# Experts: table rows made four tiles at a time, gate steps moved between the first shared units, first weight matrix split early in a job

## What is computed

```python
logits = relu(xf @ Wr1 + br1) @ Wr2 + br2
gates = softmax(logits)
tg, ti = top_k(gates, 2)
tg = softmax(tg / 2)
out = silu(xf @ Ws1 + bs1) @ Ws2 + bs2          # shared expert
for e in range(8):
    h = silu(xf @ We1[e] + be1[e]) @ We2[e] + be2[e]
    out = out + sum(tg * (ti == e)) [:, None] * h
```

## Time and profile before

| | us |
|---|---|
| median of 3 timed runs | 3277.19 (3273.32 to 3281.86) |
| profiled execution, whole | 3266.33 |
| its span (first to last instruction) | 3264.6 |
| PE busy | 2611.5 (80%) |
| DVE busy | 2268.8 (69%) |
| ACT busy | 1770.8 (54%) |
| POOL busy | 1493.4 (46%) |

### The profile page before, as it was taken

How to read it: one execution, slowest core, us unless ns; L and a number is a source line. 1 busy time by engine, 2 the same in 40 slices (tenths; PEclk the granted TensorE clock), 3 DMA queues, 4 the chain that set the end, 5 groups by cost and what they waited for, 6 DMA issues and landing times. The chain is left out here.

```text
span 3264.6 us, 38830 instructions
## 1 busy us (share of the span) xinstructions
PE 2611.5 (80%) x11128; PEld 1659.1 (51%) x11128; DVE 2268.8 (69%) x4031; ACT 1770.8 (54%) x3051; POOL 1493.4 (46%) x1600
## 2 busy tenths in 40 slices
PE   6788129989989989877788069958988888886999
PEld 5666014334334334226666057745655555553787
DVE  5477247999999999986477244557777778773443
ACT  2477036655655656523477045525777766764554
POOL 3765546887887888864764700021121112110000
PEclk7999659999999999996899579978999999997999
DMA  2045112222222222211145110000000000001000
GB/s 83 14 130 125 52 56 61 70 71 70 72 69 71 72 69 71 73 57 51 27 138 111 52 39 1 0 11 1 1 1 1 2 2 1 1 1 36 7 7 13
DMA packets 99367, 146.02 MB, mean 45 GB/s; under 512 B 12892, under 2 KB 50524, under 8 KB 98980
## 3 DMA queue, kind: packets, MB, share of 16 engines
q1 hardware_dynamic: 82052, 98.41, 9.9%
q0 software_dynamic: 16608, 44.78, 5.8%
q10 hardware_dynamic: 512, 0.53, 0.1%
HBM read 124.78 MB, written 18.87 MB: 44 GB/s over the span
## 5 line engine op out<-in xcount | busy, mean ns | idle before, releaser
L1548 POOL TENSOR_TENSOR a_hc<-a_H,a_cb 128x512 f32<-128x512 f32 x512 | 623.2, 1225 | 191.8 <-DVE a_H L1464 157.0
L1281 PE MATMUL a_Y<-a_hc,ident 128*128 128x512 f32 x1024 | 523.2, 630 | 22.8 <-POOL a_hc L1548 20.6
L1988 DVE TENSOR_REDUCE a_mx<-a_W 128x1 f32<-128x512 f32 (+3 forms) x768 | 396.1, 549 | 152.2 <-PE a_W L1792 100.0
L1894 ACT ACTIVATE a_pt<-a_W 128x512 f32<-128x512 f32 (+3 forms) x768 | 352.9, 492 | 221.5 <-PE a_W L1805 218.2
L1388 ACT ACTIVATE a_dA<-a_dt,a_aneg 128x512 f32<-128x512 f32 x512 | 338.7, 714 | 171.1 <-DVE a_H L1464 94.6
L1805 PE MATMUL a_W<-a_Q,a_K 128*128 128x512 f32 (+3 forms) x768 | 301.1, 397 | 4.8 <-issue 2.6
L1281 PEld LDWEIGHTS a_Y<-a_hc,ident 128*128 128x128 f32 x1024 | 179.4, 193 | 244.8 <-issue 128.1
L545 DVE TENSOR_TENSOR m_hl<-m_raw,m_hh 128x512 fp32r<-128x512 f32 x248 | 171.9, 694 | 172.5 <-ACT m_hh L390 158.6
L2136 POOL TENSOR_TENSOR a_spare<-a_zero 128x1 f32<-128x1 f32 x128 | 26.5, 207 | 575.1 <-ACT a_pt L1894 575.1
L1789 PE MATMUL a_W<-a_K,a_Q 128*128 128x512 f32 (+3 forms) x768 | 272.1, 361 | 11.2 <-DVE a_mx L1988 10.8
L386 ACT ACTIVATE m_raw<-m_U,m_wg 128x512 f32<-128x512 f32 x248 | 174.2, 704 | 155.0 <-PE m_U L276 138.3
(11 more groups left out here) (310 smaller groups left out, 6533.6 us busy)
## 6 DMA issues: line engine op xcount, KB each, us to landing
a_cb<-a_crow SPq DMA_DIRECT2D x256, 256.0 KB, 3.2
m_orows<-m_yt SPq DMA_DIRECT2D x46, 256.0 KB, 2.6
t_wst<-ternary_w SPq DMA_DIRECT2D x22, 256.0 KB, 2.6
m_xrows<-m_pool SPq DMA_DIRECT2D x16, 256.0 KB, 2.3
m_xg<-m_xrows,m_gidx POOLq DMA_INDIRECT x184
m_pool<-m_orows,m_didx POOLq DMA_INDIRECT x128
out<-x SPq DMA_DIRECT2D x8, 256.0 KB, 2.3
m_wg<-moe_ws SPq DMA_DIRECT2D x2, 516.0 KB, 4.4
```

Source lines behind the costliest of these rows:

```text
L1281: pe.matmul(Y[:, h, :], ident[:], hc[:, g % HCRING, :], start=False, stop=v == NS - 1).then_inc(s_y, 1)
L1548: pool.tensor_tensor(hc[:, G % HCRING, :], H[:, s, span], cb[:, v % RING, :], ALU.mult).then_inc(s_hc, 1)
L1894: act.activation(pt[:, u % PR, 0:BLK - r * P], W[:, 3 + u % 3, 0:BLK - r * P], ACT.Exp).then_inc(s_exp, 1)
L1988: dve.tensor_reduce(dst, W[:, s % 3, 0:min(BLK, (t + 1) * P - c * BLK)], AX, ALU.max)\
```

## The change

1. **Table rows.** Two instructions make four tiles' rows: an `is_equal` on DVE (128 x 384, new tile `eqa`, two buffers), then a product with the token numbers on POOL (128 x 384). The ring `oha` has three slots of four tiles, `ohb` four slots instead of three. DVE's `eqa` of group q waits for POOL's product of group q-2, POOL's product waits for `eqa`.
2. **Where groups stand.** Shared units 1 to 4 take 3, 5, 5 and 3 groups; units 5 and 6 have none, and the indices follow unit 4.
3. **Gate.** `gate` becomes `gate_top` (to the first choice) before unit 0 and `gate_second` behind the first two `hl` of unit 0. `positions` becomes `counts` (end of unit 0), `places` and `split_places` (behind the first and second `hl` of unit 1), and `experts` (behind the third group of the table). PE does `up(1)` ahead of its counting matmuls. `weights()` of DVE (the two factors of a token) goes from unit 1 to unit 2.
4. **The exponential** of the gate's difference leaves ACT: POOL computes it as a power of a constant (128 x 32).
5. **First weight loads.** POOL issues them behind its fourth product instead of ahead of all rows.
6. **First weight matrix of a job.** ACT's part goes to DVE as a copy, and both parts stand behind the first `hl` of the unit instead of at its end.

```diff
-        NWG, NXG, NYT, NXN, NOB, NOA = 4, 3, 3, 4, 3, 8
+        NWG, NXG, NYT, NXN, NOB, NOA = 4, 3, 3, 4, 4, 3
...
-        oha = pool8[:, NXN + NOB, :]
-        oha2 = sb("oha2", [P, 3 * HOT])
+        eqa, oha = sb("eqa", [P, 2, TPB, HOT]), sb("oha", [P, NOA, TPB, HOT])
...
+        root_e = sb("root_e", [P, TILES])
...
-        TABLE = {1: (0, 2), 2: (2, 5), 3: (5, 8), 4: (8, 11), 5: (11, 14), 6: (14, 16)}
+        TABLE = {1: (0, 3), 2: (3, 8), 3: (8, 13), 4: (13, 16)}
...
                 def table(i):
                     pe.wait_ge(s_ob, i // TPB + 1)
-                    pe.wait_ge(s_oa, i + 1)
+                    pe.wait_ge(s_oa, i // TPB + 1)
                     n = i % TPB
-                    pe.matmul(T[:, 0:HOT], ohb[:, i // TPB % NOB, n * P:(n + 1) * P], hot_a(i),
+                    pe.matmul(T[:, 0:HOT], ohb[:, i // TPB % NOB, n * P:(n + 1) * P], oha[:, i // TPB % NOA, n, :],
                               start=(i == 0), stop=(i == PAIRS - 1)).then_inc(s_tab, 1)
...
                 for u in range(UNITS + 2):
-                    if u < UNITS:
+                    if u < UNITS and u != 1:
                         up(u)
                     if u >= 2:
                         out_T(u - 2)
                     if u == 0:
+                        up(1)
                         positions()
...
-                def first_high(j):
-                    act.wait_ge(s_wg[j % NWG], weights_in(j))
-                    if j >= 2:
-                        act.wait_ge(s_up, KC * (SH + j - 1))
-                    act.activation(w1h[:, j % 2, :], wg[:, j % NWG, 0:BLK], ACT.Copy).then_inc(s_w1h, 1)
...
-                act.wait_ge(s_dd, 1)
-                act.activation(tt[:], dd[:], ACT.Exp, scale=0.5).then_inc(s_tt, 1)
...
-                    if SH - 1 <= u < UNITS - 1:
-                        first_high(u + 1 - SH)
...
+                def hot(q):
+                    at = slice(q * TPB, (q + 1) * TPB)
+                    wait(dve, s_oa, q - 1)
+                    dve.tensor_tensor(eqa[:, q % 2], C["iota_a"].unsqueeze(1).broadcast_to([P, TPB, HOT]),
+                                      dbase[:, at].unsqueeze(2).broadcast_to([P, TPB, HOT]), ALU.is_equal)\
+                       .then_inc(s_eq, 1)
                     wait(dve, s_tab, TPB * (q - NOB + 1))
...
-                def first_low(j):
-                    dve.wait_ge(s_w1h, j + 1)
+                def first(j):
+                    dve.wait_ge(s_wg[j % NWG], weights_in(j))
+                    if j >= 2:
+                        dve.wait_ge(s_up, KC * (SH + j - 1))
+                    step(dve.tensor_copy(w1h[:, j % 2, :], wg[:, j % NWG, 0:BLK]))
                     dve.tensor_tensor(w1l[:, j % 2, :], wg[:, j % NWG, 0:BLK], w1h[:, j % 2, :].bitcast(F32),
                                       ALU.subtract).then_inc(s_w1l, 1)
...
-                gate()
+                gate_top()
                 for u in range(UNITS + 2):
                     if SH <= u < UNITS:
                         second(u - SH)
                     for k in range(KC):
                         if u < UNITS:
                             low(u, k)
+                        if (u, k) == (0, 1):
+                            gate_second()
+                        if (u, k) == (0, 3):
+                            counts()
+                        if (u, k) == (1, 0):
+                            places()
+                        if (u, k) == (1, 1):
+                            split_places()
+                        if k == 0 and SH - 1 <= u < UNITS - 1:
+                            first(u + 1 - SH)
                         if k == 1 and u >= 2:
                             take(u - 2)
                         if k == 2 and SH - 1 <= u < UNITS - 1:
                             rows_low(u + 1)
-                    if SH - 1 <= u < UNITS - 1:
-                        first_low(u + 1 - SH)
-                    if u == 0:
-                        positions()
-                    if u == 1:
+                    if u == 2:
                         weights()
                     for q in range(*TABLE.get(u, (0, 0))):
-                        hot_b(q)
+                        hot(q)
+                        if q == 2:
+                            experts()
                     if u == max(TABLE):
                         indices()
...
-                pool.wait_ge(s_ej, 1)
-                for j in range(NWG - 1):
-                    weights(j)
-                pool.wait_ge(s_dst, 1)
-                for i in range(PAIRS):
-                    wait(pool, s_tab, i - NOA + 1)
-                    pool.tensor_scalar(hot_a(i), C["iota_a"], dbase[:, i:i + 1], C["val"][:, i:i + 1],
-                                       ALU.is_equal, ALU.mult).then_inc(s_oa, 1)
+                pool.wait_ge(s_dd, 1)
+                pool.tensor_tensor(tt[:], root_e[:], dd[:], ALU.pow).then_inc(s_tt, 1)
+                for q in range(PAIRS // TPB):
+                    val = C["val"][:, q * TPB:(q + 1) * TPB]
+                    pool.wait_ge(s_eq, q + 1)
+                    wait(pool, s_tab, TPB * (q - NOA + 1))
+                    pool.tensor_tensor(oha[:, q % NOA], eqa[:, q % 2],
+                                       val.unsqueeze(2).broadcast_to([P, TPB, HOT]), ALU.mult).then_inc(s_oa, 1)
+                    if q == 3:
+                        pool.wait_ge(s_ej, 1)
+                        for j in range(NWG - 1):
+                            weights(j)
```

More of the change, by code:

```diff
@@ L173, in moe_ffn @@
         s_M, s_pos, s_dst, s_ej = sem("M"), sem("pos"), sem("dst"), sem("ej")
-        s_ob, s_oa, s_tab, s_idx = sem("ob"), sem("oa"), sem("tab"), sem("idx")
+        s_eq, s_ob, s_oa, s_tab, s_idx = sem("eq"), sem("ob"), sem("oa"), sem("tab"), sem("idx")
         s_up, s_raw, s_hh, s_hl = sem("up"), sem("raw"), sem("hh"), sem("hl")
         s_dn, s_ye, s_yT, s_yo = sem("dn"), sem("ye"), sem("yT"), sem("yo")
-        s_w1h, s_w1l, s_w2l = sem("w1h"), sem("w1l"), sem("w2l")
+        s_w1l, s_w2l = sem("w1l"), sem("w2l")
         SHARED = NWG - 1
@@ L204, in b2 @@
             return wg[:, gslot(u), B2:B2 + 1]
-        def hot_a(i):
-            n = i % NOA
-            return oha[:, n * HOT:(n + 1) * HOT] if n < 5 else oha2[:, (n - 5) * HOT:(n - 4) * HOT]
-        TABLE = {1: (0, 2), 2: (2, 5), 3: (5, 8), 4: (8, 11), 5: (11, 14), 6: (14, 16)}
+        TABLE = {1: (0, 3), 2: (3, 8), 3: (8, 13), 4: (13, 16)}
         with nc.Block() as block:
@@ L457, in first_of_equals, with gate_top @@
                     step(dve.tensor_tensor(hot[:], c[:], bc(m), ALU.is_equal))
-                def gate():
+                def gate_top():
                     dve.wait_ge(s_lg, SH)
@@ L469, in gate, with gate_second @@
                     first_of_equals(gt, top1, eq, cc, cm, oh1)
+                def gate_second():
                     step(dve.scalar_tensor_tensor(gm[:], oh1[:], -2.0, gt[:], ALU.mult, ALU.add))
@@ L482, in weights, with counts @@
                     step(dve.tensor_tensor(wab[:, 1, :], wab[:, 0, :], tt[:], ALU.mult))
-                def positions():
+                def counts():
                     dve.wait_ge(s_pos, 1)
-                    within = T[:, 0:E * TILES].rearrange("p (t e) -> p t e", e=E)
                     step(dve.tensor_copy(tot[:], T[:, E * TILES:].rearrange("p (t e) -> p e t", e=E)))
-                    dve.wait_ge(s_cst, 3)
+                    dve.wait_ge(s_cst, 4)
                     step(dve.tensor_tensor_scan(cum[:].rearrange("p e t -> p (e t)"), ones8[:],
@@ L496, in positions, with places @@
                     step(dve.tensor_tensor_scan(cc8[:], ones8[:, 0:E], ce8[:], 0.0, ALU.mult, ALU.add))
[L498 to L502, removed]
+                def places():
+                    within = T[:, 0:E * TILES].rearrange("p (t e) -> p t e", e=E)
                     step(dve.tensor_tensor(d1[:], cc8[:], ce8[:], ALU.subtract))
@@ L509, in positions, with split_places @@
                     step(dve.tensor_tensor(gt[:], within, dst[:].rearrange("p e t -> p t e"), ALU.add))
+                def split_places():
                     step(dve.tensor_tensor(pr1[:], gt[:], oh1[:], ALU.mult))
@@ L518, in positions, with experts @@
                     dve.tensor_copy(spare[:], dmod[:, 0:1]).then_inc(s_dst, 1)
-                def hot_b(q):
+                def experts():
+                    step(dve.tensor_tensor(le[:], cc8[:].unsqueeze(1).broadcast_to([P, JOBS, E]),
+                                           C["jota"].unsqueeze(2).broadcast_to([P, JOBS, E]), ALU.is_le))
+                    step(dve.tensor_reduce(ej[:], le[:], AX, ALU.add))
+                    step(dve.tensor_scalar(ejc[:], ej[:], float(E - 1), float(P), ALU.min, ALU.mult))
+                    dve.tensor_scalar(widx[:], ejc[:], C["part"], None, ALU.add).then_inc(s_ej, 1)
+                def hot(q):
[4 more added lines that the diff above has]
+                       .then_inc(s_eq, 1)
```

(4 more changed lines are left out.)

## The result

| | us |
|---|---|
| changed kernel, median of 5 timed runs | 3253.17 (3244.30 to 3266.77) |
| kernel before, beside it | 3276.37 (3269.52 to 3281.86) |
| ratio | 0.9935, 95% interval 0.9905 to 0.9964 |
| profiled execution, whole; its span | 3254.12; 3252.4 |
| busy: PE, DVE, ACT, POOL | 2627.7 (81%), 2325.6 (72%), 1747.1 (54%), 1423.6 (44%) |

The change is faster, by 21 to 23 us, where 52 were forecast. The span is 12.2 us shorter than the one before. Unit starts tell where that comes from. Here is PE's timeline of the changed kernel, the answer to the earlier trace rows: start, duration, line (270 is `up`, 321 the table), with the idle time ahead in brackets.

The account below looks back on a forecast made before the run. No engine full throughout: DVE's small steps, POOL's table rows, then waits for the first matrix bound it in turn. 4.6 + 4.8 + 16.8 = 26.2 us a run, 52 for both, gave 3225 us; range 3188 to 3254.

Parts of the forecast that it names:

- the term for the jobs: Units 10 to 30: a job falls from 7.84 to 7.0 us, saving 16.8 us a run of the experts.
- The ring: Jobs: chain from DVE's split of the first matrix to PE and round again, 7.84 us, forecast 6.66 after edit 6.
- I can't derive this stall: Units 8 and 9: ACT's 2.76 us "remote" wait during sixteen gathers; 4.8 us gain taken there, between 1.7 and 8.0.
- POOL becomes the bound of the jobs: Rival, units 10 to 30: longer POOL issues make a job 8.28 us, the whole 3296; chance 0.04.
- The edit in the jobs doesn't bring what it says: Rival: rows' low part or DVE ends as late as the old matrix, 7.6 us a job, 3251; chance 0.14.
- a job above 7.5: Sign of being wrong, in the jobs: a job above 7.5 us with DVE waiting for weights.
- Gate and positions: Edits 3 and 4, before the table: first table instruction at 68.9, 5.2 us earlier; unit 2 ahead by 2.2.
- Table: Edits 1, 2, 5: a group takes 1.6 us, between 1.13 and about 2.0; shared units of three groups 12.4, five 15.7.
- Units 3, 4 and 5: Table's shared units: unit 3 starts near 98, lasts to 113.7; unit 4 to 126.1; gathers start at 128.1.
- Units 5 and 6: Units without table groups, ahead of unit 7: 6.0 us each by PE's work.
- Unit 7 at 138.1: Start of unit 7, 3.6 us later than before, its gathered rows already there at 135.8.
- Unit 8 at 144.9: Start of unit 8, 6.8 us after unit 7 without the idle 5.82; ahead by 4.6.

Follow-up runs that it names:

- experiment 5: Kernel before with a fifth gather a job on POOL, into a tile that nothing reads: 3337.33 us, ratio 1.0186.
- experiment 2: Changed kernel, each job gathering the rows of only two of its four tiles, so three POOL transfers in place of five: 3192.71 us, ratio 0.9749.
- edits 1 to 5 alone: Changed kernel with the split of the jobs' first weight matrix as in the kernel before: 3263.35 us, ratio 0.9969.
- experiment 8: Changed kernel, weights loaded by SP, first gathers paced: 3200.49 us, ratio 0.9829; second kernel, empty places also gathering different rows: 3187.27 us, ratio 0.9794.
- the same relief: Kernel before with weights loaded by SP, gathers waiting for the block two before, and empty places gathering rows 0 to 127: 3258.50 us, ratio 0.9948.
- experiment 6: Changed kernel with the first matrix's high part made early by ACT again, DVE making only the low part: 3247.72 us, ratio 0.9918.
- experiment 4: Changed kernel with each gathered row cut to 32 of its 128 numbers, still four gathers a job: 3272.50 us, ratio 0.9995.
- experiment 7: Changed kernel with the experts' weights loaded by SP's plain transfers, POOL keeping the gathers: 3212.73 us, ratio 0.9806.

## Why the prediction was wrong

**The failed step** is the term for the jobs: "I take 7.0, so 0.84 x 20 = 16.8 us over units 10 to 30". It measured 7.77 and 1.3 us. The ring itself was about right: jobs without a stall take 6.44 to 7.2, several of them 6.66, and 6.62 where no count is late. That it is 6.66 to the digit is partly luck, since at 6.62 PE has no gap left and its own work (6.6 by the prediction) sets the length. POOL was rightly named as what is late next. The five issues of a job took 6.9 us by the earlier trace rows and take 6.6 to 6.9 now. Wrong was to price a POOL without a pause by its issue times alone. The prediction even noted that "the 1.22 us that it now waits ahead of a load disappears". With that pause the counts came in time; without it they come about 3 us late every 15.5 us (experiment 5 shows it without the change, experiment 2 takes it away with the change in place).

**The same cause stood in the rows of before.** The 2.76 us with "remote" in the earlier trace rows fell while sixteen gathers went out. The prediction said "I can't derive this stall" and priced it as a fixed mishap of units 8 and 9, of which half might go. It was the one place in these rows that shows how this chip answers to an unbroken row of transfers. The rival "POOL becomes the bound of the jobs" had the right place, but with longer issues as the mechanism and a slower kernel (3296) as the outcome; the issues kept their 0.94 to 1.36 us. The rival "The edit in the jobs doesn't bring what it says" has the right number, 3251 with jobs of 7.6 us, and that is luck: it lets the rows' low part or DVE end too late, and where counts come in time the same order of the split gives 6.62. Of the signs of being wrong, a job above 7.5 came true, "DVE waiting for weights" did not.

**Point by point.**
- Gate and positions: first table instruction at 68.9 forecast, 69.3 measured; unit 2 at 76.9, measured 75.8. Right.
- Table: 1.6 us a group taken; measured 1.70, a product of 1.21 and 0.49 of wait. The sum used 5.1 and 8.4 us for three and five groups, where 1.6 each makes 4.8 and 8.0; the slip brought it nearer to the measurement. A product without DVE beside it took 0.83, inside the 0.8 to 0.97 worked out by length. POOL's rows, which answer to the earlier trace rows:

```profile
106.59 1.21 POOL L690 TENSOR_TENSOR m_oha<-m_eqa,m_cst 128x384 f32<-128x384 f32 x1 [0.49 <-DVE m_eqa L516]
```

```profile
L690 POOL TENSOR_TENSOR m_oha<-m_eqa,m_cst x32: 827/1208/1211, 69.9 to 1573.5; 128x384 f32<-128x384 f32 x32
```

  The rule of the Trainium skill (SBUF — State Buffer, "Who interferes with whom") that VectorE with two SBUF inputs contends with GpSimd's reads agrees with the step from 0.83 to 1.21; its full 2.0 a group did not come.
- Units 3, 4 and 5: 98, 113.7 and 126.1 forecast; 96.2, 112.8 and 126.2 measured. First gather 128.1 forecast, 127.93 measured. Right.
- Units 5 and 6: 6.0 us each by PE's work; measured 7.6 and 5.9. PE was busy all of 126 to 140 us, at a granted clock of 0.87, and unit 5's first matmuls took 0.77 and 0.63 us against 0.47 and 0.39 in the jobs. The sum had left the clock out here.
- Unit 7 at 138.1; measured 139.8. Unit 8 at 144.9; measured 151.2. The rows did come in time, but the stall of the burst moved into unit 7, as this wait of ACT's eviction shows (with edits 1 to 5 alone it is 5.7 us), and unit 8 starts 1.7 us later than before instead of 4.6 earlier:

```profile
142.06 0.94 POOL L662 DMA_INDIRECT m_xg<-m_xrows,m_gidx  x1 [0.30 <-issue]
145.11 0.69 ACT L371 ACTIVATE m_ysb<-m_Y,m_wg 128x512 f32<-128x512 f32 x1 [4.42 <-remote]
```

- Units 8 and 9: 17.2 us by the forecast, 13.1 measured. With edits 1 to 5 alone they take 15.7, since the stall had been paid already; edit 6 takes off the other 2.6. So at unit 10 forecast and measurement differ by 2.2 us only (9.4 ahead against 7.2): the errors of units 8 to 10 cancel, which is luck.
- The rule that a cast on VectorE keeps GpSimd from writing descriptors (same page and section of the Trainium skill) would have made 0.2 us of the third cast. No row shows it: the gather that starts with the cast of 231.93 took 0.95, the next one, with no cast beside it, 1.36.

The error is then 15.5 us in the jobs of the first run and 2.2 ahead of them, 17.7 of the 26.2 us forecast for it. With counts no longer late, what is the change worth? The second kernel of experiment 8 is 2.1% faster than the kernel before (1.9 to 2.2), but the kernel before gains 0.5% from the same relief. The difference, 1.5% or 50 us, is the 52 that were forecast. The posts of these two kernels give 71 us, so whether the change is then worth more than the forecast is not shown.

## What to carry to other kernels

When an edit takes away the last pause of an engine that issues indirect transfers, don't price that engine by the length of its issues: look in the trace of before for a place where it already issues without a pause, and for waits that no instruction explains there. Give that engine fewer transfers (loads whose address is one number can go to SP) before shortening the ring around it. And let places that hold nothing read different rows.

## What the runs showed of the hardware

- Counts of TensorE reached ACT and DVE late towards the end of unbroken rows of indirect transfers on POOL. The longest waits ended 1.3 us (237.04 to 238.36) to 2.1 us (143.00 to 145.11) after the row; shorter ones ended inside it (140.00, in the row from 127.93 to 143.00). How many transfers went out before ACT began to wait for a late count was not fixed: in the changed kernel it was in the eighth or ninth of most rows and in the fourteenth of one (1.25 to 1.33 us for each), in experiment 6 in the nineteenth (1.41). Rows of four with pauses of 1.5 us (experiment 8) had none, nor had rows of five with pauses of 1.2 in the kernel before. Why the counts are late is not shown, nor whether counts of other engines are.
- A quarter of the bytes for each gather didn't take the late counts away (experiment 4), and the same bytes with the weights issued by SP had none in the jobs (experiment 7).
- Loads issued by SP with the row number read from SBUF replaced POOL's indirect ones at no cost that the posts show: jobs of 6.62 with PE busy 79.94 of 80.00 us. The Trainium skill (Perfetto Trace Analysis, "DMA Optimizations") says that balancing transfers over the issuing engines may help where writing descriptors is the bound. The runs agree, though POOL's issues (6.66 to 6.90 us a job) were hardly longer than the ring (6.62), and the gain (1.15 us a job) was larger than that difference.
- Gathers of one row by nearly all places took 4.4 times the DMA time of the same bytes from 128 rows (81.1% against 18.4% of the engines in 260 to 265 us).
- Where every job runs without a stall, the granted clock stays at its upper level (1.00 in 180 to 260 us), against 0.98 over the jobs of the changed kernel.
